# Second layer of a graph network: edge frames through PSUM, the head's products two portions later, four gather buffers, one bank for columns

## The reference, cut to what matters

```python
R = relu(edge_weight[:, None] @ w1 + b1) @ w2 + b2     # radial weights of every edge
Y = spherical_harmonics(rel_vec)                       # of the edge's direction
Fj = features[src]                                     # 8 scalars and 8 vectors of 3
for each pair of in and out order, each path lf:
    acc = acc + norm * einsum('euv,ef,evi,ofi->euo', R_k, Y_f, F_b, C)
out = zeros.at[dst].add(concat of acc)
x = layernorm(x + out)
```

## Time and profile before

| | us |
|---|---|
| median of 3 runs (18427.23 to 18430.5) | 18428.42 |
| the profiled execution | 18441.06 |
| its span, first to last instruction | 18439.3 |
| busy in the whole span: PE / DVE / POOL / ACT | 12519.4 / 11147.9 / 11894.6 / 2930.3 |
| second layer's loop, first to last step's start | 6644.96 to 11009.76 |

### The profile page before, as it was taken

How to read it: one execution, slowest core, us unless ns; L and a number is a source line. 1 busy time by engine, 2 the same in 40 slices (tenths; PEclk the granted TensorE clock), 3 DMA queues, 4 the chain that set the end, 5 groups by cost and what they waited for, 6 DMA issues and landing times. The chain is left out here.

```text
span 18439.3 us, 300421 instructions
## 1 busy us (share of the span) xinstructions
PE 12519.4 (68%) x95607; PEld 6807.1 (37%) x95607; DVE 11147.9 (60%) x19696; ACT 2930.3 (16%) x5512; POOL 11894.6 (65%) x10055
## 2 busy tenths in 40 slices
PE   0466555555555557777777773667666665999999
PEld 0344443433333334444444441222222222455554
DVE  2465554444444469999999995333333335577776
ACT  0122222222222211111111110111111110000000
POOL 4788888888888867777777767777777774000000
PEclk6565555555555578888888886777777667999999
DMA  8333333333333342222222224544554553799998
GB/s 313 48 37 39 38 39 39 38 38 37 38 36 38 36 65 61 62 63 63 62 63 63 63 55 47 92 88 87 90 91 86 90 91 89 227 288 292 299 289 263
DMA packets 3002798, 1816.44 MB, mean 99 GB/s; under 512 B 1734093, under 2 KB 2760210, under 8 KB 2983410
## 3 DMA queue, kind: packets, MB, share of 16 engines
q1 hardware_dynamic: 2206148, 1338.06, 29.3%
q0 software_dynamic: 669312, 166.80, 12.9%
q10 hardware_dynamic: 126512, 300.38, 4.7%
HBM read 1475.61 MB, written 392.90 MB: 101 GB/s over the span
## 5 line engine op out<-in xcount | busy, mean ns | idle before, releaser
L2017 POOL DMA_INDIRECT xg<-d_tab,s_i x3136 | 3333.5, 1063 | 1122.4 <-issue 579.9
L2567 POOL DMA_INDIRECT xg<-d_tab,s_i x3136 | 2994.4, 955 | 957.9 <-issue 903.0
L1403 POOL DMA_INDIRECT d_acc<-AG,ix x1568 | 2472.5, 1577 | 527.2 <-issue 466.2
L1403 POOL DMA_INDIRECT d_acc<-T,ix x1568 | 2466.7, 1573 | 478.2 <-issue 445.6
L2953 PE MATMUL pacc<-nodes,HB 128*32 128x512 fp8e4 x47040 | 2664.7, 380 | 41.2 <-PEq L2997 40.8
L1756 PE MATMUL pm<-ms,eq 128*128 128x32 f32 x6272 | 1367.7, 400 | 896.1 <-PEq L1754 896.1
L2604 DVE TENSOR_TENSOR_SCAN U<-mU,U,up 128x512 f32<-128x512 f32 x392 | 501.4, 1279 | 2368.1 <-DVEq L2603 2365.5
L2953 PEld LDWEIGHTS pacc<-nodes,HB 128*32 128x32 f16 x47040 | 1258.8, 97 | 1320.0 <-issue 58.1
L1756 PEld LDWEIGHTS pm<-ms,eq 128*128 128x128 f32 x6272 | 1345.3, 330 | 940.5 <-issue 940.2
L2295 PE MATMUL pR<-w,H 64*128 64x384 f32 x6272 | 1539.4, 569 | 0.0
L1035 PE MATMUL pw<-ok,ol 128*128 128x392 bf16 x4048 | 1302.3, 457 | 299.9 <-PEq L1033 299.8
(11 more groups left out here) (345 smaller groups left out, 18938.0 us busy)
## 6 DMA issues: line engine op xcount, KB each, us to landing
packed<-d_A SPq DMA_DIRECT2D x420, 1792.0 KB
row<-d_m SPq DMA_DIRECT2D x1568, 64.0 KB
xg<-d_tab,s_i POOLq DMA_INDIRECT x6272
wrow<-d_w SPq DMA_DIRECT2D x392, 256.0 KB
d_scan<-so ACTq DMA_DIRECT2D x392, 256.0 KB
d_A<-stage ACTq DMA_DIRECT2D x97, 784.0 KB
d_ea<-in_ea_t ACTq DMA_DIRECT2D x1, 50176.0 KB, 230.7
d_exp<-T ACTq DMA_DIRECT2D x1, 50176.0 KB, 252.6
```

Of the source, the lines that this page charges most:

```text
L1403: e.indirect_dma_start(out=d_acc[i], out_offset=bass.IndirectOffsetOnAxis(ap=ix[k][:, t:t + 1], axis=0), in_=mo[k][:, t * F:(t + 1) * F], ...
L2017: e.indirect_dma_start(out=xg[k][:, t, :], out_offset=None, in_=d_tab, in_offset=bass.IndirectOffsetOnAxis(ap=s_i[n][:, t:t + 1], axis=0)) ...
L2567: e.indirect_dma_start(out=xg[n][:, j * ST + c, :], out_offset=None, in_=d_tab, in_offset=bass.IndirectOffsetOnAxis(ap=s_i[d][:, col:col + ...
```

## The change

The frames no longer go to DVE from SBUF. ACT copies the frame of portion n from `e9[n]` into half k of a PSUM bank `framed` (`frames`), as soon as the frame is loaded and DVE has made the tail product of portion n - 2 (`feP`), and then lets the head have it and SP load the next (`give`, behind `hidden` in ACT's queue). Head and tail product read it there as their second operand. The head is called after products 4 in place of products 2. `xg` gets four buffers for two. The bank for `framed` comes from `tp`, which has one bank for two: columns, scan, columns back and their copy-out share it, and `columns` waits for the copy-out of the portion before. The diff's core:

```diff
-            xg = [sb(st, f"xg{k}", [P, T, F]) for k in range(2)]
+            xg = [sb(st, f"xg{n}", [P, T, F]) for n in range(DEEP)]
...
-            tp = [ps(edges, f"tp{j}", [P, SW]) for j in range(2)]
+            tp = [ps(edges, "tp", [P, SW])]
+            framed = ps(edges, "framed", [P, 2, 3, T, 3])
+            eP = [framed[:, k, :, :, :] for k in range(2)]
...
-                        e.wait_ge(S(f"le{n}"), 16)
-                        e.sem_inc(S(f"le{n}"), -16)
-                        of = xg[n % 2][:, :, 8:32].rearrange("p t (v i) -> p t v i", i=3)
+                        e.wait_ge(S(f"eP{n % 2}"), 1)
+                        e.sem_inc(S(f"eP{n % 2}"), -1)
+                        of = xg[n][:, :, 8:32].rearrange("p t (v i) -> p t v i", i=3)
                         for i in range(3):
-                            last = e.tensor_tensor(hp[:, i, :, :, :], bc(of[:, :, :, i], 1, 3), bc(e9[n][:, :, :, i], 3, 8),
+                            last = e.tensor_tensor(hp[:, i, :, :, :], bc(of[:, :, :, i], 1, 3), bc(eP[n % 2][:, :, :, i], 3, 8),
                                                    ALU.mult)
...
-                            e.tensor_tensor(tv[:, :, :, :, :], bc(Q[k][:, 1:4, :, :], 4, 3), bc(e9[n][:, :, :, :], 3, 8),
+                            e.tensor_tensor(tv[:, :, :, :, :], bc(Q[k][:, 1:4, :, :], 4, 3), bc(eP[k], 3, 8),
                                             ALU.mult).then_inc(S("tz"), 1)
                         elif part == 1:
                             e.wait_ge(S("tz"), 1)
                             e.sem_inc(S("tz"), -1)
+                            e.sem_inc(S(f"feP{k}"), 1)
...
-                            if u == 2 and not last:
+                            if u == 4 and not last:
                                 head((n + 1) % 4, count)
...
+                    def frames(n):
+                        k = n % 2
+                        e.wait_ge(S(f"le{n}"), 16)
+                        e.sem_inc(S(f"le{n}"), -16)
+                        e.wait_ge(S(f"feP{k}"), 1)
+                        e.sem_inc(S(f"feP{k}"), -1)
+                        e.activation(eP[k], e9[n][:, :, :, :], ACT.Copy).then_inc(S(f"eC{k}"), 1)
+
+                    def give(n):
+                        e.wait_ge(S(f"eC{n % 2}"), 1)
+                        e.sem_inc(S(f"eC{n % 2}"), -1)
+                        e.sem_inc(S(f"eP{n % 2}"), 1)
+                        e.sem_inc(S(f"fe{n}"), 1)
...
                             scalars(n % 2)
+                            frames((n + 2) % 4)
                             hidden((n + 2) % 4)
+                            give((n + 2) % 4)
                             early_sums((n + 1) % 2)
                             spread((n + 2) % 4)
                             scan_store(e, b, it * 4 + n, n % 2)
...
-                        e.sem_inc(S(f"fe{n}"), 1)
                         e.sem_inc(S(f"ff{k}"), 1)
-                        e.wait_ge(S(f"fpb{k}"), 1)
-                        e.sem_inc(S(f"fpb{k}"), -1)
+                        e.wait_ge(S("fpb0"), 1)
+                        e.sem_inc(S("fpb0"), -1)
                         for j in range(CH):
-                            last = e.transpose(tp[k][:, j * P:(j + 1) * P],
+                            last = e.transpose(tp[0][:, j * P:(j + 1) * P],
...
-                            last = e.transpose(b["pb"][k][:, j * ST:(j + 1) * ST, :], b["sc"][k][:, j * P:(j + 1) * P],
+                            last = e.transpose(b["pb"][0][:, j * ST:(j + 1) * ST, :], b["sc"][k][:, j * P:(j + 1) * P],
```

More of the change, by code:

```diff
@@ L1997, in _ @@
                 def _(e):
+                    for n in range(DEEP):
+                        e.sem_inc(S(f"fxg{n}"), 1)
                     for k in range(2):
-                        e.sem_inc(S(f"fxg{k}"), 1)
                         e.sem_inc(S("half"), 1)
                     def gathers(n, group):
-                        k = n % 2
                         e.wait_ge(S(f"li{n}"), 16)
                         e.sem_inc(S(f"li{n}"), -16)
-                        e.wait_ge(S(f"fxg{k}"), 1)
-                        e.sem_inc(S(f"fxg{k}"), -1)
+                        e.wait_ge(S(f"fxg{n}"), 1)
+                        e.sem_inc(S(f"fxg{n}"), -1)
                         for t in range(T):
@@ L2016, in gathers @@
                                 e.sem_inc(S("past_" + e.engine.name), 1)
-                            e.indirect_dma_start(out=xg[k][:, t, :], out_offset=None, in_=d_tab,
+                            e.indirect_dma_start(out=xg[n][:, t, :], out_offset=None, in_=d_tab,
                                                  in_offset=bass.IndirectOffsetOnAxis(ap=s_i[n][:, t:t + 1], axis=0)
@@ L2133, in scan @@
                     def scan(n):
-                        scan_dve(e, b, n, tp[n % 2][:, :], ALU.mult, ALU.add)
+                        scan_dve(e, b, n, tp[0][:, :], ALU.mult, ALU.add)
                         e.sem_inc(S(f"fmg{n % 2}"), 1)
@@ L2205, in spread @@
                         e.sem_inc(S(f"ff{k}"), -1)
-                        e.activation(FG[k][:, :, 0:8], xg[k][:, :, 0:8], ACT.Copy).then_inc(S("ca"), 1)
+                        e.activation(FG[k][:, :, 0:8], xg[n][:, :, 0:8], ACT.Copy).then_inc(S("ca"), 1)
                         e.activation(FG[k][:, :, 8:16], turned[:, 0, :, :], ACT.Copy).then_inc(S("ca"), 1)
@@ L2234, in scalars @@
                                      ACT.Copy).then_inc(S("ms"), 1)
+                    frames(0)
+                    frames(1)
+                    give(1)
+                    give(0)
                     hidden(0)
@@ L2249, in _ @@
                         scalars(n)
+                        frames(n + 2)
                         hidden(n + 2)
+                        give(n + 2)
                         early_sums(1 - n)
@@ L2337, in back @@
                         for j in range(CH):
-                            last = e.transpose(b["pb"][k][:, j * ST:(j + 1) * ST, :], b["sc"][k][:, j * P:(j + 1) * P],
+                            last = e.transpose(b["pb"][0][:, j * ST:(j + 1) * ST, :], b["sc"][k][:, j * P:(j + 1) * P],
                                                ident[:, :])
-                        last.then_inc(S(f"pb{k}"), 1)
+                        last.then_inc(S("pb0"), 1)
                     def step(n, past=2, last=False):
```

## The result

The changed kernel takes 18279.99 us (median of 4 runs, 18277.03 to 18283.93) against 18427.82 of the kernel before beside it: a ratio of 0.992, 95% interval 0.990 to 0.994.

What follows compares the result with a forecast made beforehand. It took POOL's gather rate for the bound, 22.35 us a step. With POOL at 21.2, DVE's 21.54 + 0.10 = 21.64 sets the step: 144 us and 4 in the first wait, 148 gained, 18280 us; range 18200 to 18345.

Steps and rivals of the forecast that it cites:

- The bound: Second layer's loop: POOL's gather rate sets the step, 22.35 us of a measured 22.38; DVE is next, 0.84 us behind.
- The prediction's sum for POOL: Second layer, 16 gathers a step: undisturbed time and gap 19.90 us, holds 1.92, further idle time 0.53; together 22.35.
- POOL waiting for half in most steps: Sign expected in the profile of after: POOL's queue waits for `half` in most steps of the second layer.
- (1): Head and tail product reading the frame from PSUM take 1.14 us a step from POOL, leaving 21.2.
- (2): DVE's own durations in head and tail product: gain taken as 0, at most 0.27 us for the head products.
- (3): Head moved from the third product to the fifth: gives 4 us once, in the first wait, nothing per step.
- (4): Head no longer covers PE's sums between radials 3 and 4: products 4 wait 0.1 us a step, bounds 0 and 0.3.
- Rival B: PE, at the low clock, becomes the bound at products 4: step 22.79 us, slower at 18504 us; chance 0.10.
- (5): New waits for ACT's frames and the columns' shared bank, SP's earlier queue, four xg buffers: all costed at 0.
- A: POOL stays the bound: length or place of DVE's lines holds gathers, not the SBUF operand; 18424 us, chance 0.08.
- C: More gain on DVE: a head product takes a plain sum's 557 ns; 18227 us, chance 0.10.

Runs made afterwards that it cites:

- later head alone: Kernel before, with only the head called behind products 4 in place of products 2; 18385.72 us, ratio 0.996.
- tail only: Changed kernel, but the head reads its frame from SBUF as before and only the tail product from PSUM; 18326.39 us, ratio 0.994.
- head only: Changed kernel, but the tail product reads its frame from SBUF as before and only the head from PSUM; 18342.34 us, ratio 0.995.
- 17 gathers: Changed kernel with one more gather for each portion, into a tile that nobody reads; 18524.57 us, ratio 1.003.
- late loads: Changed kernel with one more gather per portion and SP's frame buffer given free by PE at the columns again; 18347.85 us, ratio 0.995.
- other order: Changed kernel with one more gather per portion and SP issuing frame, flags, weights, indices, not weights, indices, frame, flags; 18406.98 us, ratio 0.999.

## Why the prediction was right, point by point

- **The bound: right, on an argument weaker than it looked.** The prediction's sum for POOL meets the measured step: 22.35 for 22.38 (before), 22.02 for 22.05 (later head alone), 21.83 for 21.86 (tail only), 21.93 for 21.95 (head only), and with 17 gathers 22.79 for 22.78, 21.89 for 21.92 (late loads) and 22.16 for 22.19 (other order). But busy and idle time make up the step for any engine; in the changed kernel, where DVE is the bound, the same sum gives 21.54 for 21.65. What tells the bound is who waits. In these seven kernels the head, where it waits, starts a median of 1.67 to 1.74 us behind the end of its last gather, and POOL's queue is held by `half` in 3 steps of some 190 at most. In the changed kernel POOL leads by 17 us and is held. The prediction's sign "POOL waiting for half in most steps" came in 92 of 194 steps, nearly all in the second half of the loop.
- **(1) What PSUM operands relieve: right in kind, too small.** I took 1.14 us a step and left 0.73 with the tail sums. The hold fell from 1.92 to 16 x (0.973 - 0.944) = 0.46, by 1.46. One step's rows could not show the gathers that were held through a tail sum and the head together, 3.04 us. The rule of the Trainium skill that I set against it, "SBUF — State Buffer", section "Who interferes with whom", by which a tensor_tensor leaves descriptor generation alone (inferred, as the page says itself), does not hold here: a gather takes up to 3.04 us beside lines with two SBUF operands, and 0.94 to 0.96 beside head and tail product once they have one in PSUM.
- **(2) DVE's durations: right.** Head 648 to 642 ns, tail product 1355 to 1349.
- **(3) "A later deadline does not mend a rate": the sentence holds, the term was wrong.** The first wait shrank from 10.24 to 6.16 us, the 4 us of the sum. But the move also changes which lines stand side by side, and alone it is worth 0.33 us a step, not 0. In the changed kernel this counts for nothing, since the frames in PSUM have already freed the head's gathers.
- **(4) The lost cover: right.** I had 0.1 us a step from a third of the steps at some 0.3 us; it is 19.7 us in 65 steps, 0.1 a step, and 0 where the head stands ahead of products 4 again. Rival B's clock did not come: radial 4 ran at a granted clock of 1.00 in the stalled step shown.
- **(5) Costs of 0: right for ACT, the shared bank and the buffers, wrong for SP.** The shared bank and the frames delayed no one on DVE. PE waits 0.8 us for the head in 130 steps ahead of its turn, without effect on DVE. But "all of SP's queue runs earlier", which I priced at 0, costs POOL 1.18 - 0.53 = 0.65 us a step in idle time. With it POOL's sum is 19.90 + 0.46 + 1.18 = 21.54 us, not 21.2. Some of the 1.18 is waiting for `half` late in the loop, but two other readings agree that POOL has only about 0.1 us to spare under DVE's 21.65: the 17th gather found 0.1, and POOL's lead grew by 0.13 a step. Two errors of a third and two thirds of a microsecond met below the bound: the relief too small by 0.32, the landings by 0.65. That they did not reach it is luck: had they been 0.15 us worse, the time would have moved with them.
- **Rivals.** A falls as stated, though the half of it that speaks of place is true of the kernel before. C did not come: the head product kept its price.

## What to carry to other kernels

Where an engine issues indirect gathers back to back, split its time (undisturbed duration, gap, holds, waits for landings) before calling the busier-looking engine the bound. The sum meets the step for any engine; what names the bound is that none of its idle time is a wait for another engine's work, and that the next engine starts as soon as its last piece has landed. Here, moving one operand of a vector line to PSUM freed the gathers beside it, and only lines with both operands in SBUF held them. When a semaphore is given earlier, look at the whole queue that waits on it: each load behind it changes its place too.

## What the runs showed of the hardware that I had not expected

One gather can be held by several vector lines in a row (3.04 us for 0.94). And with 17 gathers a step and the same 848 KB of SP's loads, the gathers' idle time beyond 0.30 us each was 0.45, 0.64 or 1.27 us a step, depending on the order and place of those loads alone.
